# Reordering the slots of a fused two-layer block on one Trainium2 core: batches 0 to 3 first, routing cut into pieces, attention steps later in a slot

## What is computed

```python
xn = _layernorm(x)
x = x + linear_attention(xn) + fp6_linear(xn)              # layer 0
xn = _layernorm(x)
x = x + attention_over_batches(xn) + mixture_of_experts(xn)  # layer 1
...
q, k, v = (t.reshape(8, 512 * 16, 8).transpose(1, 0, 2) for t in (q, k, v))
attn = softmax(einsum('nqd,nkd->nqk', q, k) * 8 ** -0.5)    # 8 x 8 for each token position and head
...
scores = sigmoid(x @ w_gate.T)                              # 16 experts in 4 groups
allowed = best 2 groups by the sum of their 2 best; then the best 4 experts; w = w / (w.sum() + 1e-06)
routed = sum over e of combine[t, e] * (silu(x @ w1_e.T) * (x @ w3_e.T)) @ w2_e.T   # + a shared expert
```

## Time and profile before

| | us |
|---|---|
| median of 3 runs (lowest, highest) | 407.57 (407.36, 408.72) |
| the profiled execution | 408.92 |
| its span, first to last instruction | 407.1 |
| TensorE matmul busy | 323.2 |
| VectorE busy | 344.1 |
| ScalarE busy | 188.4 |
| GpSimd busy | 235.4 |

### The profile page before, as it was taken

How to read it: one execution, slowest core, us unless ns; L and a number is a source line. 1 busy time by engine, 2 the same in 40 slices (tenths; PEclk the granted TensorE clock), 3 DMA queues, 4 the chain that set the end, 5 groups by cost and what they waited for, 6 DMA issues and landing times.

```text
span 407.1 us, 5016 instructions
## 1 busy us (share of the span) xinstructions
PE 323.2 (79%) x1455; PEld 237.0 (58%) x1455; DVE 344.1 (85%) x831; ACT 188.4 (46%) x501; POOL 235.4 (58%) x149
## 2 busy tenths in 40 slices
PE   0267696898898875805129999999999999999995
PEld 0136475777787765704016666666666666666662
DVE  3774997987887964599999899999999999999791
ACT  0535556778678656702122262624426262442521
POOL 9151573553644721095065959778695986867450
PEclk9986998999999999775758999999999999999999
DMA  7620000100100102220000000000000000000000
GB/s 184 209 77 1 2 0 1 54 37 17 52 22 32 53 27 96 91 52 0 1 0 1 2 0 27 2 26 0 0 28 1 26 2 26 1 2 26 0 26 27
DMA packets 13247, 12.49 MB, mean 31 GB/s; under 512 B 1548, under 2 KB 9924, under 8 KB 13220
## 3 DMA queue, kind: packets, MB, share of 16 engines
q1 hardware_dynamic: 10944, 10.10, 7.7%
q0 software_dynamic: 736, 0.95, 1.2%
q10 hardware_dynamic: 1540, 1.12, 0.9%
HBM read 5.88 MB, written 2.10 MB: 20 GB/s over the span
## 4 chain that ended last, share of the span: by engine, by line
PE 54%; DVE 19%; ACT 11%; issue 7%; POOL 6%; DMA 1%; ACTq 1%; POOLq 0%; DVEq 0%
PE Q L833 18%; PE VK L833 16%; PE T L833 9%; PE ND L833 6%; PE T L829 4%; ACT xn L546 4%; POOL prod_qk L773 3%; POOL prod_pv L783 2%; PE Q L829 2%; ACT qkv L503 1%; DMA headmask<-in_c_headsel 1%; ACT Q L585 1%; DVE chosen L1411 1%; DVE bst L1086 1%; DVE scr L1341 1%
## 5 line engine op out<-in xcount | busy, mean ns | idle before, releaser
L783 POOL TENSOR_TENSOR prod_pv<-prob,qkv 128x1024 f32<-128x1024 f32 x32 | 69.6, 2212 | 45.0 <-DVE att L1358 24.3
L686 ACT ACTIVATE sg<-Q 128x512 f32<-128x512 f32 x72 | 43.2, 599 | 97.7 <-PE Q L833 95.0
L773 POOL TENSOR_TENSOR prod_qk<-qkv 128x1024 f32<-128x1024 f32 x32 | 75.9, 2397 | 16.7 <-DVE scr L1341 16.7
L833 PE MATMUL VK<-hid,w 128*128 128x512 f32 x144 | 74.5, 599 | 0.0
L833 PE MATMUL Q<-xT_hi,w_hi 128*128 128x512 f32 x72 | 52.3, 726 | 0.7 <-ACT combT L672 0.7
L1441 DVE TENSOR_TENSOR sgc<-ND,sg 128x512 f32<-128x512 f32 x64 | 43.6, 681 | 6.7 <-PE ND L833 4.7
L1454 DVE TENSOR_TENSOR hid<-T,sgc 128x512 f32<-128x512 f32 x64 | 43.5, 679 | 0.3
L833 PE MATMUL T<-xT_hi,w_hi 128*128 128x512 f32 x72 | 28.9, 401 | 17.0 <-DVE hid L1454 17.0
L833 PE MATMUL Q<-bias,ones 128*128 128x384 f32 (+1 forms) x64 | 32.8, 512 | 9.4 <-ACT qkv L503 5.8
L1341 DVE TENSOR_REDUCE scr<-prod_qk 128x128 f32<-128x1024 f32 x32 | 38.4, 1205 | 0.0
L1358 DVE TENSOR_REDUCE att<-prod_pv 128x128 f32<-128x1024 f32 x32 | 38.2, 1195 | 0.0
(11 more groups left out here) (190 smaller groups left out, 796.9 us busy)
## 6 DMA issues: line engine op xcount, KB each, us to landing
xT_hi<-xTs_hi SPq DMA_DIRECT2D x8, 256.0 KB, 2.3
xT_lo<-xTs_lo SPq DMA_DIRECT2D x8, 256.0 KB, 2.3
out_x<-fin SPq DMA_DIRECT2D x8, 256.0 KB, 2.3
x<-in_x SPq DMA_DIRECT2D x2, 256.0 KB, 4.7
wraw<-in_w1T SPq DMA_DIRECT2D x1, 512.0 KB, 10.8
w<-in_w2T SPq DMA_DIRECT2D x1, 512.0 KB, 4.6
wraw<-in_w3T ACTq DMA_DIRECT2D x1, 512.0 KB, 3.1
sel<-in_c_sel POOLq DMA_DIRECT2D x4, 128.0 KB, 2.8
```

The source lines that it names most:

```text
L686: act.activation(sg[:, side(half, s), :], QB[side(half, s)][:, :], ACT.Silu).then_inc(sg_ready, 1)
L773: pool.tensor_tensor(prod_qk[:, t % 2], bc(qkv2[:, TH * half + t, j, 0:D], 1, NB), qkv2[:, :, j, D:2 * D], ALU.mult).then_inc(qk_prod, 1)
L783: pool.tensor_tensor(prod_pv[:, t % 2].rearrange("p (h e) b -> p b h e", e=HD), bc(prob[:, t], 3, HD), qkv2[:, :, j, 2 * D:QKV].rearrange( ...
L833: return pe.matmul(o, lhsT, rhs, start=start, stop=stop)
```

## The change

- Slots take j = n % 4 and half = n // 4: batches 0 to 3 in slots 0 to 3, then batches 4 to 7. TensorE waits for `comb2` of the first half inside slice 0 of slot 0, and for the second half in slot 3, slice 6.
- `route` is cut into seven pieces. Of the first half, two pieces go into step 10 and two into step 11 of stage one, the other three behind it. Of the second half, the pieces stand in slots 0 (s = 5, 7), 1 (s = 4, 8), 2 (s = 4, 8) and 3 (s = 1). `comb2` now lies in `wraw`.
- `sigmoid(0)` moves to step 10 on ScalarE (and a dummy square root brings the other table back); the low parts of w1 and w3 and the zeroing and loading of `sel` move to GpSimd in steps 9 and 10.
- In a slot VectorE has scores 2 and 3 at s = 0 and 1, `less_max` at s = 2, `sum_of_p` at s = 3, `over_sum` at s = 4, the next slot's scores 0 and 1 at s = 3 and 5, `values` at s = 5 to 8. Slot 0 has an order of its own. ScalarE's exponential moves from s = 1 to s = 2 (slot 0: s = 4). GpSimd has `normalise` before its last `product_qk`, not after it.
- `scr` and `prob` become [row, head, batch].

```diff
-                slot(n, n // 2, n % 2)
+                slot(n, n % NJ, n // NJ)
...
-        scr = sb("scr", [P, 2, TH, NB, H])
+        scr = sb("scr", [P, 2, TH, H, NB])
-        prob = sb("prob", [P, TH, NB, H])
+        prob = sb("prob", [P, TH, H, NB])
...
+                if at(i, STEPS - 2):
+                    sigmoid(0)
...
                     if s == 1:
-                        exp_done(n, half)
                         yT_evac(n)
-                    if at(n, 0) and s == COMB_SLICE:
+                    if s == (4 if n == 0 else 2):
+                        exp_done(n)
...
             def step(i):
                 run(i, 1, mx_over_scale)
                 run(i, 3, residual)
+                if i == STEPS - 3:
+                    low_part(w1_lo[:, :], wraw[:, :], w1_hi[:, :], w1_hi_ready, w1_ready)
+                    sel_padded()
+                if i == STEPS - 2:
+                    low_part(w3_lo[:, :], wraw[:, :], w3_hi[:, :], w3_hi_ready, w3_ready)
...
                 products_pv(n, j)
                 next_qk(2)
+                normalise(n)
                 next_qk(3)
-                normalise(n)
...
                 if at(i, STEPS - 1):
-                    low_part(w3_lo[:, :], wraw[:, :], w3_hi[:, :], w3_hi_ready, w3_ready)
+                    route_allowed(0)
+                    route_top(0)
...
+                if at(i, STEPS - 2):
+                    route_pairs(0)
+                    route_ranks(0)
...
             pipeline(dve, step)
-            route(0)
-            scores(0, 0, 0)
-            scores(0, 1, 0)
-            route(1)
-            scores(0, 2, 0)
-            scores(0, 3, 0)
+            route_chosen(0)
+            route_weights(0)
+            route_parts(0)
...
+            def first_slot(s):
+                if s < TH:
+                    scores(0, s)
+                if s == TH:
+                    less_max(0)
+                if s == 6:
+                    sum_of_p(0)
+                    scores(1, 0)
+                if s == 8:
+                    scores(1, 1)
+                    over_sum(0)
+                    dve.wait_ge(xT_kept, 32 * NB)
+                    for t in range(TH):
+                        values(0, t)
+
+            def later_slot(n, s):
+                more = follow(n) is not None
+                if s < 2:
+                    scores(n, 2 + s)
+                if s == 2:
+                    less_max(n)
+                if s == 3:
+                    sum_of_p(n)
+                    if more:
+                        scores(n + 1, 0)
+                if s == 4:
+                    residual(n - 1)
+                    over_sum(n)
+                if s == 5 and more:
+                    scores(n + 1, 1)
+                if s >= NS - TH:
+                    values(n, s - (NS - TH))
```

More of the change, by code:

```diff
@@ L406, in slots, with side, follow @@
             for n in range(NSLOT):
[L407 to L424 removed]
+                slot(n, n % NJ, n // NJ)
+        COMB_SLOT, COMB_SLICE = NJ - 1, 6
+        def side(n, s):
+            return (n + s) % 2
+        def follow(n):
+            return None if n == NSLOT - 1 else ((n + 1) % NJ, (n + 1) // NJ)
         def blocks(t):
@@ L479, in exp_of, with run @@
         def exp_of(act):
-            def run(n, half):
+            def run(n):
                 act.wait_ge(s_sub, n + 1)
@@ L759, in residual, with low_part, sel_padded @@
                 pool.tensor_tensor(x[:, c], x[:, c], l0_sum[:, :, :], ALU.add).then_inc(x1_ready, 1)
+            def low_part(dst, src, hi, hi_ready, ready):
+                pool.wait_ge(hi_ready, 1)
+                pool.tensor_tensor(dst, src, f32(hi), ALU.subtract).then_inc(ready, 1)
+            def sel_padded():
+                pool.wait_ge(qkv_rope, NT)
+                pool.wait_ge(rope_sum, NB)
+                pool.memset(f32(sel[:, :, :, :]), 0.0).then_inc(sel_zeroed, 1)
+                pool.wait_ge(sel_zeroed, 1)
+                for j in range(NJ):
+                    pool.dma_start(sel[2 * NE * j:2 * NE * (j + 1), j], d["c_sel"]).then_inc(ld_sel, 16)
             def step(i):
@@ L808, in slot @@
             def slot(n, j, half):
-                nxt = follow(n, j, half)
+                nxt = follow(n)
                 def next_qk(t):
@@ L1045, in slot @@
                     after(pe, sg_ready, NS * n + s - 1)
-                    g = QB[side(half, s)]
+                    g = QB[side(n, s)]
                     mm(g[:, :], w1_hi[:, w], hi, True, False)
@@ L1049, in slot @@
                     mm(g[:, :], w1_lo[:, w], hi, False, True).then_inc(g_ps, 1)
+                    if n == 0 and s == 0:
+                        comb_transposes(0)
                     after(pe, hid_ready, NS * n + s - 1)
-                    u = UB[side(half, s)]
+                    u = UB[side(n, s)]
                     mm(u[:, :], w3_hi[:, w], hi, True, False)
@@ L1332, in step, with scores @@
                     vu_sum()
-            def scores(n, t, half):
+            def scores(n, t):
                 u = TH * n + t
@@ L1455, in hidden, with residual, route_later @@
                     .then_inc(hid_ready, 1)
-            def residual(n, j, half):
+            def residual(n):
+                j, half = n % NJ, n // NJ
                 dve.wait_ge(yback_ps, n + 1)
                 dve.wait_ge(fin_free, n + 1)
-                V.tensor_tensor(fin[:, half], x[:, TH * half:TH * half + TH, j, :], tiles(Q2), ALU.add)\
+                V.tensor_tensor(fin[:, n % 2], x[:, TH * half:TH * half + TH, j, :], tiles(Q2), ALU.add)\
                     .then_inc(fin_ready, 1)
+            def route_later(n, s):
+                if (n, s) == (0, 5):
+                    route_pairs(1)
+                if (n, s) == (0, 7):
+                    route_ranks(1)
+                if (n, s) == (1, 4):
+                    route_allowed(1)
+                if (n, s) == (1, 8):
+                    route_top(1)
+                if (n, s) == (2, 4):
+                    route_chosen(1)
+                if (n, s) == (2, 8):
+                    route_weights(1)
+                if (n, s) == (3, 1):
+                    route_parts(1)
@@ L1464, in slot @@
             def slot(n, j, half):
-                first = isinstance(n, int) and n == 0
-                nxt = follow(n, j, half)
-                before = (n - 1, j, 0) if half else (n - 1, j - 1, 1)
                 for s in range(NS):
-                    if s == 2:
-                        if nxt is not None:
-                            scores(n + 1, 1, nxt[1])
-                        sum_of_p(n)
-                    weighted(n, s, side(half, s))
-                    if s == 0:
-                        less_max(n, half)
-                    if s in (1, 7, 8) and nxt is not None:
-                        scores(n + 1, {1: 0, 7: 2, 8: 3}[s], nxt[1])
-                    if s == 3:
-                        over_sum(n)
-                    if 3 <= s < 3 + TH:
-                        values(n, s - 3)
-                    if s == 4 and not first:
-                        residual(*before)
-                    hidden(n, s, side(half, s))
+                    weighted(n, s, side(n, s))
@@ L1486, in _ @@
+                    if n == 0:
+                        first_slot(s)
+                    else:
+                        later_slot(n, s)
+                    route_later(n, s)
+                    hidden(n, s, side(n, s))
             slots(dve, slot)
-            residual(NSLOT - 1, NJ - 1, 1)
+            residual(NSLOT - 1)
 def constants():
```

149 lines of the change are left out of this document (73 added, 76 removed).

## The result

| | before | after |
|---|---|---|
| median (lowest, highest), us | 407.78 (407.36, 408.72) | 447.39 (444.31, 451.54) |
| the profiled execution, us | 408.92 | 448.42 |
| its span, us | 407.1 | 446.5 |
| VectorE busy, us | 344.1 | 340.3 |
| TensorE matmul busy, us | 323.2 | 338.6 |

The change makes the kernel slower by 9.2%: the ratio is 1.092, with a 95% interval of 1.087 to 1.097. One of the four executions of the changed kernel, 451.54, was in a slower state of the chip, which no ratio here counts; the median of the other three is 446.4, and that is the figure used from here on. The forecast was 435, with a range of 415 to 446. So direction and mechanism held, the size was 11 us short, and the time lies at the upper end of the range, 0.4 us beyond it by this median (the ratio times the 407.57 of before gives 445.1).

A forecast was written before the change was run, and what follows sets the result against it. Bound before by two routing holes on TensorE, then by slots with TensorE and VectorE near full. Slots 251.1 us against 200.6 (+50.5), start -22.3, net +28.2 on 407.57: 435 us, range 415 to 446.

The forecast's parts named there:

- The start: First sgc of slot 0 at 184.2 us, 22.3 us earlier than before (bounds 18.5 and 26).
- The cost at nothing: Low parts of w1 and w3 and sel, moved to GpSimd in stage one, were costed at zero.
- where I had counted 3 us: Allowance behind stage one for routing steps running beside GpSimd's first two products: 3 us (0 to 5).
- The exponential's wait: In each later slot, VectorE idles 2.0 us at slice 3 because silu 3 stands behind the exponential.
- the wait for `att`: At each slot's end, TensorE idles 3 us before the transposes, waiting for GpSimd's normalise.
- gate product to gate product: Length of a steady slot between first gate products: 29.0 us against 23.97 before (bounds 25.8 or 27.0, and 30.0).
- the sign of being right: Slots 4 to 6 would take 28 to 30 us from first gate product to first gate product.
- the clock: TensorE's clock behind the slot-end pauses: it need not fall, so nothing was added for it.
- the third rival: TensorE falls to 1.2 GHz behind each pause: +1.5 us a slot, total 445; chance 0.10.
- That TensorE sets the slot at 25.8: Rival: new waits overlap and VectorE catches up, 25.8 us a slot, total 409; chance 0.11.
- The faster case: Rival: the routing's gain is kept, slots stay at 24.0 us with att ready within 25.4, total 398; chance 0.13.
- the case in which they are everywhere: If GpSimd never paused, port collisions would make slots 0 to 3 some 5 us longer than the sum.

The follow-up runs named there:

- run 3: Changed kernel with TensorE's transposes of att moved behind slice 0 of the next slot, ScalarE's copy behind the first silu there; 427.6 us, ratio 1.047.
- run 4: Changed kernel with the attention steps of slots 1 to 7 back in their old places, slot 0 making two more scores; 422.6 us, ratio 1.034.
- Run 1: Changed kernel with twelve dummy matmuls on TensorE before its wait for att at each slot's end; 442.1 us, ratio 1.079.
- run 9: The kernel of run 8 with the second half's ranks and weights moved from slice 1 to slice 3 of slots 1 and 3; 400.0 us, ratio 0.977.
- run 10: Changed kernel's stage one, layout and first half, but second half of routing as one block ahead of slot 0, old slot order and steps; 400.5 us, ratio 0.979.
- run 8: Changed kernel with old step order, late transposes, held first products, slot 0's values spread and routing pieces at other places; 404.4 us, ratio 0.990.

## Why the prediction was short

**The start**: forecast 184.2, measured 186.38. The low part of w3, which I had moved to GpSimd at no cost, ran on it from 161.83 for 2.65 us, and a piece's step `cmp_eq` took 2.71 us from 162.04, which put `xTs_lo` of batch 6 at 165.25:

```profile
161.59 0.42 DVE L1412 TENSOR_TENSOR cmp_eq<-gs 128x256 f32<-128x256 f32 x1
162.04 2.71 DVE L1413 TENSOR_TENSOR cmp_eq<-cmp_eq,tri 128x256 f32<-128x256 f32 x1
```
```profile
161.83 2.65 POOL L756 TENSOR_TENSOR w_lo<-wraw,w_hi 128x1152 fp32r<-128x1152 f32 x1 [1.34 <-ACT w_hi L515]
```

The cost at nothing was wrong: I looked for who waits for w3, and not for what runs beside it. That this overlap is the cause is read from the rows; no run takes it back. `xTs_lo` of batch 7 ended at 173.2, where I had 172.0. Two steps behind stage one then met the products, where I had counted 3 us; it was 4.1 (2.50 and 2.31 us for 0.42 and 0.29).

**The mechanism** was right in each part that can be read off. The exponential's wait is 2.01 us (forecast 2.0), the wait for `att` 3.08 (3), gate product to gate product in slot 4, at a granted clock of 1.00, is 347.76 - 318.84 = 28.92 us (29.0), slots 1 to 3 took 30.65, 32.20 and 32.40 (30.7, 31.4, 31.5), the reductions of the new layout took 676 ns (685). Slots 5 and 6, 30.51 and 30.54 us at a clock of 0.94, lie above the 28 to 30 that I had named as the sign of being right. Runs 3 and 4 confirm the cause by removing it: late transposes 26.5, old order 23.8.

**The term that was mis-sized** is the clock, which I put at zero with "it need not" fall, arguing from stage one, where PE is busy 115.73 of 157 us at 0.96. Slots 4 to 6 took 91.0 us together against a forecast of 87, and slot 7 34.7 against 32.5. Run 1 takes the fall of the clock away and gives 87.0 and 32.7. I had the case as the third rival, +1.5 a slot and a total of 445, and gave it 0.10. It was half right: the fall came behind some pauses and not behind others, so forecast and rival were parts of one case, and a range to 446 gave it little room. The mean over a stage with short idle times did not tell what one pause of 3 us does.

**The remainder.** By the profile the 11.2 us between the forecast's span of 435.3 and 446.5 are: start 2.2, slot 0 1.2 (39.2 against 38.0), slots 1 to 3 1.7 (95.3 against 93.6), slots 4 to 6 4.0, slot 7 2.2. What remains in slots 0 to 3 was not followed up. A last 0.8 us is arithmetic: 407.57 + 28.2 is 435.8, and I wrote 435.

**The other rivals.** That TensorE sets the slot at 25.8 is excluded: the slot was 28.92 at the full clock, and even with the chain at its end taken away (run 3) it was 26.5. The faster case needed `att` within 25.4 us of a slot's start; it came at 346.22 + 1.08 - 318.84 = 28.5. Its other half, that the routing's gain can be kept, holds only in part, and with other orders: runs 9 and 10 are 8 to 9 us faster than the kernel before, 4.1 of them the layout's, where the start alone was forecast to give 22.3.

**The pages.** The exponential's idle time of 2.01 us carries no further drain behind the table load, as the load and silu of the earlier trace rows had it; by the Trainium skill, "ScalarE: Activation LUTs", What ACT_TABLE_LOAD costs, which adds a drain of about 1380 ns to a load, I estimate that it would have been 3.4; the measurement decides. The collisions with products I had counted only where my layout met one, and put 5 us more on the case in which they are everywhere. The rows of runs 4, 8 and 9 decide: the same `cmp_eq` takes 2.27 us beside a product and 0.42 without, and run 9 gained 5.1 us by avoiding that in two places. This is as the Trainium skill, "SBUF — State Buffer", Who interferes with whom, has it: a VectorE operation with two SBUF inputs and a GpSimd one that reads SBUF exclude each other. The score reductions stayed at 1.21 us beside products, and in run 4 MAX8 at 1.31 (1.32 clear of them) and the replacement at 0.16.

## What to carry to other kernels

When an edit empties a hole by spreading its work over a steady stage, first ask which engine of that stage has room, and then what runs on GpSimd at the very place: here small steps of 8.5 us in clean time cost nearly 20 in slots 1 to 3, which were full (run 4), and 10.25 us of them cost 13.4 once most of them stood where GpSimd waited (run 9). And look at the last chain of a stage before moving anything in it later: `values`, `normalise`, transposes and gate product had 0.05 us to spare, and with the clock's part it cost 3.8 us in every steady slot. Where the last link (the transposes) can be taken one slice later, as in run 3, the chain gets slack back.
